# Split tables made once, and the mix as one plain fp32 product of identity plus matrix

## The reference, cut to what matters

```
x: (64 sequences, 32 channels, 512); adapter: (64,), values 2..6; cond: (64,), values 0..15

def lora_add(base, inp, A, B):            # A (16, 16, in), B (16, out, 16), one of 16 adapters per sequence
    Ab, Bb = A[0][adapter], B[0][adapter]
    t = einsum('bri,bni->bnr', Ab, inp)
    return base + einsum('bor,bnr->bno', Bb, t) * 0.5
gate = lora_add(x @ W_gate.T, x, A_gate, B_gate)      # 512 -> 1376
up   = lora_add(x @ W_up.T,   x, A_up,   B_up)
act  = silu(gate) * up
h    = x + lora_add(act @ W_down.T, act, A_down, B_down)   # 1376 -> 512
out  = h + einsum('bct,bcd->bdt', h, weights[cond])   # weights (16, 32, 32): mixes the 32 channels of a sequence
```

## Time and profile before

| | us |
|---|---|
| median of 3 runs | 447.93 (446.21 to 448.08) |
| profiled execution, its own time | 446.79 |
| its span, first to last instruction | 445.0 |
| TensorE busy | 438.1 (98%) |
| VectorE busy | 335.2 (75%) |
| ScalarE busy | 212.3 (48%) |
| POOL (GpSimd) busy | 169.7 (38%) |

### The profile page before, as it was taken

How to read it: one execution, slowest core, us unless ns; L and a number is a source line. 1 busy time by engine, 2 the same in 40 slices (tenths; PEclk the granted TensorE clock), 3 DMA queues, 4 the chain that set the end, 5 groups by cost and what they waited for, 6 DMA issues and landing times.

```text
span 445.0 us, 7248 instructions
## 1 busy us (share of the span) xinstructions
PE 438.1 (98%) x2475; PEld 393.5 (88%) x2475; DVE 335.2 (75%) x623; ACT 212.3 (48%) x397; POOL 169.7 (38%) x156
## 2 busy tenths in 40 slices
PE   8989999999999999999999999999999999999997
PEld 6877888888888888888888888999999999999996
DVE  6779999878867867857857858978667767766665
ACT  6746355366444544543543444843454454444531
POOL 2722223121121221121121452675776666756620
PEclk9999999999999999999999999999999999999999
DMA  8975664356555665665565599947776665556631
GB/s 243 381 242 146 181 172 114 109 172 188 145 181 151 159 172 145 161 173 144 159 173 144 145 287 340 247 138 202 215 201 208 208 180 178 177 178 196 191 96 47
DMA packets 99843, 81.12 MB, mean 182 GB/s; under 512 B 50944, under 2 KB 83200, under 8 KB 99808
## 3 DMA queue, kind: packets, MB, share of 16 engines
q1 hardware_dynamic: 88512, 47.27, 37.9%
q0 software_dynamic: 11008, 33.30, 24.8%
q10 hardware_dynamic: 288, 0.10, 0.1%
HBM read 65.18 MB, written 15.47 MB: 181 GB/s over the span
## 4 chain that ended last, share of the span: by engine, by line
PE 92%; DMA 2%; POOL 2%; issue 2%; DVE 1%; ACT 1%; SPq 0%; POOLq 0%
PE bank L1384 28%; PE bank L1262 9%; PE bank L1263 9%; PE bank L1261 9%; PE bank L1216 7%; PE bank L1217 7%; PE bank L1218 7%; PE bank L1283 4%; PE bank L1284 4%; PE bank L1414 2%; POOL a_raw L453 2%; PE bank L1394 2%; DMA b_raw<-in_b_rows,rows 2%; DMA gu_landing<-in_w_gate 1%; PE bank L1399 1%
## 5 line engine op out<-in xcount | busy, mean ns | idle before, releaser
L453 POOL DMA_INDIRECT b_raw<-in_b_rows,rows x48 | 51.8, 1078 | 188.7 <-DVE b_gu L803 188.1
L1384 PE MATMUL bank<-wd,actT_hi 128*128 128x288 f32 (+1 forms) x636 | 109.9, 295 | 0.0
L1384 PEld LDWEIGHTS bank<-wd,actT_hi 128*128 128x128 f32 (+1 forms) x636 | 93.8, 188 | 1.4 <-issue 0.2
L453 POOL DMA_INDIRECT a_dn_raw<-in_a_dn_rows,rows x64 | 77.3, 1208 | 19.5 <-issue 19.5
L803 DVE SCALAR_TENSOR_TENSOR b_gu<-b_raw,low_rows,b_gu 128x1024 fp32r<-128x1024 f32 (+1 forms) x48 | 55.6, 1159 | 26.8 <-ACT b_gu L513 26.8
L1384 PE MATMUL bank<-wd,actT_lo 128*128 128x288 f32 (+1 forms) x318 | 68.1, 296 | 0.0
L513 ACT ACTIVATE b_gu<-b_raw 128x1024 fp32r<-128x1024 f32 (+1 forms) x48 | 46.2, 963 | 11.2 <-DMA b_raw<-in_b_rows,rows 9.8
L1384 PEld LDWEIGHTS bank<-wd,actT_lo 128*128 128x128 f32 (+1 forms) x318 | 51.0, 188 | 0.0
L603 ACT ACTIVATE act<-bank 128x512 f32<-128x512 f32 (+1 forms) x48 | 26.1, 546 | 41.4 <-PE bank L1284 41.4
L910 DVE TENSOR_TENSOR act<-act,bank 128x512 f32<-128x512 f32 (+1 forms) x48 | 29.8, 621 | 8.6 <-PE bank L1284 7.8
L799 DVE TENSOR_TENSOR actT_lo<-actT_raw,actT_hi 128x1280 fp32r<-128x1280 f32 (+1 forms) x32 | 27.0, 886 | 11.6 <-ACT actT_hi L513 11.6
(11 more groups left out here) (180 smaller groups left out, 1004.2 us busy)
## 6 DMA issues: line engine op xcount, KB each, us to landing
actT_raw<-actT_dram SPq DMA_DIRECT2D x16, 640.0 KB
actT_dram<-staging SPq DMA_DIRECT2D x64, 128.0 KB, 2.9
x_sb<-in_x SPq DMA_DIRECT2D x16, 256.0 KB, 2.9
xT_raw<-in_xT SPq DMA_DIRECT2D x15, 256.0 KB, 2.7
out<-out_sb SPq DMA_DIRECT2D x15, 256.0 KB
a_raw<-in_a_gu_rows SPq DMA_DIRECT2D x56, 64.0 KB, 2.7
actT_dram<-staging SPq DMA_DIRECT2D x32, 88.0 KB, 3.2
wd_raw<-in_w_down SPq DMA_DIRECT2D x10, 256.0 KB, 5.9
```

Of the source, the lines that this page charges most:

```text
L453: return pool.indirect_dma_start(dst, None, src, bass.IndirectOffsetOnAxis(ap=rows[:, tile, col:col + 1], axis=0))
L1384: last = pe.matmul(ps_down[e][half][:, 0:HALF], a[e][0:n, c, :], wd[0:n, c, part, at:at + HALF], start=(c == 0 and i == 0), stop=(c == NC ...
```

## The change

Three tables are made in DRAM while stage one runs. `a_table` has for each adapter's A rows of down the hi part and the lo part side by side (1408 bytes a row), `b_table` has hi rows of B in its first half and lo rows in its second, and `mix_table` has each mix matrix plus the identity. They are made in seven rounds: four for A, two for B, one for mix. A round is a load by SP into `a_dn_raw[0]`, a copy on ScalarE into `a_dn_raw[1]`, a subtraction on VectorE in place, and two stores by SP; the mix round has no copy and adds the identity. Rounds 0 and 1 stand in pair 3, 2 and 3 in pair 4, 4 and 5 in pair 5, 6 in pair 6. The first round of a pair stands before `split_b(pr,2,0)` on ScalarE and VectorE, the second after `split_b(pr,2,1)`. The load of a round waits until the stores of the one before it have landed. The first A gather waits for all stores.

In stage two the A rows of tiles 2 to 15 are gathered from `a_table` into `a_pair` (which lies over `b_raw` and part of `b_gu`) and copied into `wd` by two ScalarE copies; VectorE no longer takes part. B rows are gathered from `b_table` straight into `b_dn`, now double, once `down_lora` of the tile two before is through. The mix matrices are loaded by SP, four DMAs of 32x32 with a register load each, straight onto the diagonal blocks of `mix_w`. The mix is one plain fp32 product of `mix_w` and the unsplit h in `x_sb`; its result is out itself, which ScalarE copies to `out_sb` (`copy_out`). The mask's minus sign is turned at the start of stage two.

```diff
+A_ROUNDS = ADAPTERS // TILE_SEQS
+ROUNDS = A_ROUNDS + 3
+FIRST_ROUNDS = 3
...
+    a_table = nc.dram_tensor("a_table", (ADAPTERS * P, 2 * A_DN), F32, kind="Internal").ap()
+    b_table = nc.dram_tensor("b_table", (2 * ADAPTERS * RANK, H), F32, kind="Internal").ap()
+    mix_table = nc.dram_tensor("mix_table", (ADAPTERS * CH, CH), F32, kind="Internal").ap()
...
+        with ExitStack() as then:
+            a_pair = [sb(f"a_pair{e}", [P, TILE_SEQS, 2 * A_DN], F32, then) for e in range(2)]
...
-        mix_raw = [sb(f"mix_raw{e}", [P, CH]) for e in range(2)]
-        mix_hi = sb("mix_hi", [P, P], F32R)
-        mix_lo = sb("mix_lo", [P, P], F32R)
+        mix_raw = sb("mix_raw", [P, CH])
+        mix_w = [sb(f"mix_w{e}", [P, P]) for e in range(2)]
...
+        b_dn = [sb(f"b_dn{e}", [P, H], F32R) for e in range(2)]
...
+        def table_parts(i):
+
+            if i < A_ROUNDS:
+                raw, to = slice(0, TILE_SEQS * A_DN), slice(TILE_SEQS * i * P, TILE_SEQS * (i + 1) * P)
+                return raw, [a_table[to, part * A_DN:(part + 1) * A_DN].rearrange("(a p) n -> p a n", p=P)
+                             for part in range(2)]
+            if i < A_ROUNDS + 2:
+                r0 = (i - A_ROUNDS) * P
+                return slice(0, H), [b_table[part * ADAPTERS * RANK + r0:part * ADAPTERS * RANK + r0 + P, :]
+                                     for part in range(2)]
+            return slice(0, TILE_SEQS * CH), [mix_table.rearrange("(a p) n -> p a n", p=P)]
...
+        def rounds_of(pr):
+
+            return [i for i in (2 * (pr - FIRST_ROUNDS), 2 * (pr - FIRST_ROUNDS) + 1) if 0 <= i < ROUNDS]
...
+            def load_round(i):
+                reached(sp, tables_stored, 32 * i)
+                if i < A_ROUNDS:
+                    sp.dma_start(a_dn_raw[0][:, :, :], a_round(i)).then_inc(table_landed, 16)
+                elif i < A_ROUNDS + 2:
+                    r0 = (i - A_ROUNDS) * P
+                    sp.dma_start(table_sb(0, slice(0, H)), b_dn_rows[r0:r0 + P, :]).then_inc(table_landed, 16)
+                else:
+                    sp.dma_start(table_sb(0, slice(0, TILE_SEQS * CH), CH),
+                                 mix_rows.rearrange("(a p) n -> p a n", p=P)).then_inc(table_landed, 16)
+                    sp.dma_start(table_sb(0, slice(TILE_SEQS * CH, (TILE_SEQS + 1) * CH)), eye)\
+                        .then_inc(table_landed, 16)
+
+            def store_round(i):
+                cols, tables = table_parts(i)
+                n = A_DN if i < A_ROUNDS else H if i < A_ROUNDS + 2 else CH
+                sp.wait_ge(table_ready, i + 1)
+                for part, to in enumerate(tables):
+                    src = table_sb(1 - part if i < ROUNDS - 1 else 0, cols, n if len(to.shape) == 3 else None)
+                    sp.dma_start(to, src).then_inc(tables_stored, 16)
+
+            def load_mix(m, e):
+                reached(sp, mix_done, 2 * (m - 1))
+                for q in range(TILE_SEQS):
+                    r = slice(q * CH, (q + 1) * CH)
+                    col = 2 * TILE_SEQS + 2
+                    row = sp.value_load(rows[q * CH:q * CH + 1, m, col:col + 1], min_val=0, max_val=(ADAPTERS - 1) * CH)
+                    sp.dma_start(mix_w[e][r, r], mix_table[bass.ds(row, CH), :]).then_inc(mix_landed[e], 16)
...
+                if rounds:
+                    load_round(rounds[0])
...
                     spill(pr, s)
+                    if s < len(rounds):
+                        store_round(rounds[s])
+                    if s + 1 < len(rounds):
+                        load_round(rounds[s + 1])
...
             sp.wait_ge(s_used, FAST)
             load_x(0, 0)
             load_actT(2, 0)
+            sp.wait_ge(tables_stored, 32 * ROUNDS - 16)
+            load_mix(0, 0)
             load_x(1, 1)
             load_actT(3, 1)
+            load_mix(1, 1)
...
+                if m == 0 and q0 == 0:
+                    pool.wait_ge(tables_stored, 32 * ROUNDS - 16)
+                if m == 2:
+                    for t in range(2):
+                        pool.wait_ge(section_done[t], NS * PAIRS)
+                reached(pool, a_dn_copied, m - 3)
                 for q in range(q0, q1):
-                    gather(a_dn_raw[m % 2][:, q, :], a_dn_rows, m, TILE_SEQS + 1 + q).then_inc(a_dn_landed[m % 2], 16)
+                    to, table = (a_dn_raw, a_dn_rows) if m < 2 else (a_pair, a_table)
+                    gather(to[m % 2][:, q, :], table, m, TILE_SEQS + 1 + q).then_inc(a_dn_landed[m % 2], 16)
...
+                reached(pool, down_lora_done, 2 * (m - 1))
+                gather(b_dn[m % 2][:, :].bitcast(F32), b_table, m, 2 * TILE_SEQS + 1).then_inc(b_dn_landed[m % 2], 16)
...
+            gather_b_dn(1)
             for m in range(2, TILES):
                 gather_a_dn(m)
-                pool.wait_ge(down_done, m - 1)
-                gather_b_dn(m - 1)
-                gather_mix(m - 1)
-            gather_b_dn(TILES - 1)
-            gather_mix(TILES - 1)
+                gather_b_dn(m)
...
+            def split_round(i):
+
+                if i == ROUNDS - 1:
+                    return
+                sc.wait_ge(table_landed, 16 * (i + 1))
+                cols, _ = table_parts(i)
+                hi(table_sb(1, cols).bitcast(F32R), table_sb(0, cols)).then_inc(table_hi_ready, 1)
...
                 split_b(pr, 2, 1)
+                for i in rounds_of(pr)[1:2]:
+                    split_round(i)
...
+                    for part in range(2):
+                        of = a_pair[e][:, :, part * A_DN:(part + 1) * A_DN]
+                        last = hi(wd_a(part, e), of.rearrange("p q (c r) -> p q c r", c=NC))
+                    last.then_inc(a_dn_copied, 1)
...
+            def copy_out(m, e):
+                sc.wait_ge(mix_done, 2 * (m + 1))
+                reached(sc, stored[e], 16 * (m // 2))
+                hi(out_sb[e][:, :], ps_mix[:, 0:H]).then_inc(out_ready, 1)
...
                 split_td(2 * j - 1)
-                split_mix(2 * j - 1, 1)
-                if j == 1:
-                    split_h(2 * j - 1, 1)
-                    split_a_dn(2 * j + 1, 1)
-                else:
-                    split_a_dn(2 * j + 1, 1)
-                    split_h(2 * j - 1, 1)
+                split_a_dn(2 * j + 1, 1)
                 split_actT(2 * j + 1, 1)
-                split_b_dn(2 * j, 0)
+                copy_out(2 * j - 1, 1)
                 split_td(2 * j)
-                split_mix(2 * j, 0)
                 split_a_dn(2 * j + 2, 0)
-                split_h(2 * j, 0)
                 split_actT(2 * j + 2, 0)
-                split_b_dn(2 * j + 1, 1)
+                copy_out(2 * j, 0)
...
+            def split_round(i):
+
+                if i == ROUNDS - 1:
+                    ve.wait_ge(table_landed, 16 * (ROUNDS + 1))
+                    to = table_sb(0, slice(0, TILE_SEQS * CH), CH)
+                    ones_ = a_dn_raw[0][:, 0:1, TILE_SEQS * CH:(TILE_SEQS + 1) * CH]
+                    nc.vector.tensor_tensor(to, to, ones_.to_broadcast([P, TILE_SEQS, CH]), ALU.add)\
+                        .then_inc(table_ready, 1)
+                    return
+                cols, _ = table_parts(i)
+                ve.wait_ge(table_hi_ready, i + 1)
+                lo(table_sb(0, cols).bitcast(F32R), table_sb(0, cols), table_sb(1, cols)).then_inc(table_ready, 1)
...
                 add_u7(pr, 1)
+                for i in rounds_of(pr)[0:1]:
+                    split_round(i)
                 split_b(pr, 2, 0)
                 if not last:
                     split_a(pr + 1, 0)
@@ -1008,12 +1084,14 @@
                 if not last:
                     split_x(pr + 1, 1)
                 split_b(pr, 2, 1)
+                for i in rounds_of(pr)[1:2]:
+                    split_round(i)
                 if not last:
                     sum_x(pr + 1)
...
+            def turn_mask():
+
+                for q in range(TILE_SEQS):
+                    c = 2 * q * RANK
+                    last = nc.vector.memset(mask[q * CH:(q + 1) * CH, c:c + RANK], LORA_SCALE)
+                last.then_inc(mask_turned, 1)
+                ve.wait_ge(mask_turned, 1)
...
-                                            ALU.add).then_inc(h_summed, 1)
-                for half, (cols, at) in enumerate(down_halves(e)):
-                    ve.wait_ge(h_hi_ready, 2 * m + half + 1)
-                    lo(h_lo[:, cols], x_sb[e][:, cols], h_hi[:, cols]).then_inc(h_ready, 1)
...
+                                            ALU.add).then_inc(h_ready, 1)
...
-            def mix_products(out_, cols):
-                pe.matmul(out_, mix_hi[:, :], h_hi[:, cols], start=True, stop=False)
-                pe.matmul(out_, mix_lo[:, :], h_hi[:, cols], start=False, stop=False)
-                return pe.matmul(out_, mix_hi[:, :], h_lo[:, cols], start=False, stop=True)
-
             def mix(m):
-                pe.wait_ge(mix_ready, m + 1)
+                e = m % 2
```

(5 more changed lines are left out.)

141 lines of the change are left out of this document (49 added, 92 removed).

## The result

| us | before | after |
|---|---|---|
| median of runs on one chip | 447.72 (446.21 to 448.08, 4 runs) | 462.23 (460.06 to 462.55, 4 runs) |
| profiled execution, its own time | 446.79 | 460.06 |
| its span | 445.0 | 458.0 |

The ratio after to before is 1.0326, 95% interval 1.0289 to 1.0364: slower. The forecast was 459.9, range 451 to 468. The profiled execution is the fastest of the kernel after, with a mean granted clock of 0.999; its others have spans of 460.2 to 461.2 us at 0.992 to 0.996. The medians are 14.5 us apart and the two profiled spans 13.0; the profiles can account for the 13.0.

A forecast was written before the change was run, and what follows sets the result against it. TensorE was taken to bound the kernel. Mix 2.7, table-round stalls 8.25 and down-stage start 1.0 made 12.0 us on the profiled 446.79, so 458.8; the median lies 1.1 above, giving 459.9 us, range 451 to 468.

The forecast's parts named there:

- The bound: Whole kernel: TensorE, busy 98% of the span, sets the time; work taken off VectorE and ScalarE gives nothing back.
- The mix: Down tiles: one plain fp32 product for three single-pass ones, +0.16 to +0.20 us a tile, +2.7 us over fifteen tiles.
- Slot A at zero: First round of a pair, before split_b(pr,2,0): its load lands before VectorE comes, 2.0 us of cover, cost 0.
- Slot B, three stalls: Second round of pairs 3, 4, 5: waiting for stores, then load, stalls the next pair's lora 3.3, 3.3, 1.65 us; +8.25 us.
- T: Moment the second round's table load lands in pair 3, 151.7; b ready at 160.4, stall T - 148.4 = 3.3 us.
- The wait at tile 2: Start of the down stage: fourth A gather 1.25 us later, b_dn(1) put in front; stall 0 to 2.0, taken as +1.0 us.
- The steady down stage at zero: Later down tiles: removed work lies beside TensorE, added gathers and DMAs are hidden; slack 2.1 us, cost 0.
- a sign of being wrong: Down stage: the forecast is wrong if ScalarE waits for a_pair in each tile and TensorE behind it.
- Hidden rounds: Gate/up pairs: landing is short or VectorE makes up more, so the table rounds cost nothing; 450.9 us, chance 0.13.
- late gathers: Down stage: gathers land 3 us later than taken, 0.9 over the slack on 13 tiles; about 12 us more, 472; chance 0.10.
- the third rival: Down stage: 288-column matmul spacing shrinks as ScalarE and VectorE traffic goes, 12 us back; 439 with rounds hidden; chance 0.05.

The follow-up runs named there:

- experiment 1: Kernel after without the load, copy and subtraction of each pair's second round, its stores kept and issued with the first round's: 455.74 us, ratio to before 1.0162.
- experiment 4: Kernel after with each pair's second round moved into the next pair, its stores ahead of load_a: 460.10 us; with 32 unused words 458.20; SP's queue also split, 455.23 and 454.09.
- experiment 5: Kernel after with the gather of b_dn(1) issued behind tile 2's A-row gathers and nothing else changed: 465.22 us, one execution.

## Why the prediction was right, point by point

**The bound.** Right: TensorE sets the time throughout, and 49 us less VectorE work bought nothing.

**The mix.** Predicted 0.16 to 0.20 per tile, 2.7 in all. The chain of a down tile after answers to the earlier trace rows:

```profile
324.61 0.49 PE bank L1445 x4
325.11 3.17 PE bank L1435 x24
328.28 0.86 PE bank L1453 x2
329.14 5.57 PE bank L1435 x42
334.71 0.48 PE bank L1445 x4
```

The mix takes 0.86 instead of 0.70, the doubled rate of the earlier trace rows without the 0.04 that I added for instruction starts; over the whole stage tiles are 10.09 us apart instead of 9.92. So it is 0.16 to 0.17 per tile and 2.4 to 2.5 in all, the low end of my bounds. Alone on the kernel before it measured 1.8 by the ratio, 2.5 by the span.

**Slot A at zero.** Right, and shown by experiment 1. It stayed true only while its load landed ahead of VectorE; in experiment 4 it did not.

**Slot B, three stalls.** The mechanism is the predicted one, row by row. Pair 3 begins 1.10 us later than before, so in the frame of before T is 152.70 - 1.10 = 151.6; predicted 151.7. Its two parts were each off by 0.6 to 0.7, in opposite directions: the store leg took 3.8 (4.5 predicted), the load leg 4.0 (3.4). That T comes out to 0.1 us is partly luck. b was ready at 161.37 - 1.10 = 160.3 (160.4). The stall beyond a quiet pair is 2.94, not 3.3, since the quiet pair is itself 0.5 longer; with the forms put back it is 3.18. The term that was mis-sized is pair 5's, 0.40 for 1.65. There SP's rows are

```profile
217.78 0.81 SPq L404 DMA_DIRECT2D b_table<-a_dn_raw  x2
220.45 0.34 SPq L391 DMA_DIRECT2D a_dn_raw<-in_b_dn_rows  x1
```

and the copy starts at 223.57: two legs of 2.7 and 3.1, 2.0 us less than the A rounds' 7.8, where I had taken 0.9 less for the smaller transfers. The A rounds also store in pieces of 704 bytes and the B rounds in pieces of 2 KB; whether that is the difference was not tried. Sum 6.3 for 8.25.

The Trainium skill, page DMA: Bandwidth & Descriptors, section Anatomy of one DMA, has about 2.0 us plus bytes at 436 GB/s, in a section on DMAs that GpSimd issues (these two are SyncE's). By it T was 150.3 and the stalls 4.4. The A legs were slower than that by 1.3 us, and the stalls, 6.3, lie between its figure and mine.

**The wait at tile 2.** Predicted +1.0 (0 to 2.0), measured 0.72, and 0.9 to 2.0 in the five variants of the kernel after that keep the order of the gathers. The price is right. In all of these the fourth A gather leaves 11.4 us after the first b_dn gather and TensorE is through with tile 1 at 19.8; what differs is the time from that gather to ScalarE's copy, 4.7 us in the kernel after and 4.9 to 5.9 in the others, within the 3.7 to 5.9 of the earlier trace rows. The reason given for the later gather, b_dn(1) ahead of it, is not right: experiment 5 takes it away and nothing is won. By the rows of POOL what makes it late is the wait of the first A gather for the last lora product together with POOL's hold; no run separates the two.

**The steady down stage at zero.** Right, with less room than the prediction gave it. ScalarE waits for A rows in nearly every tile, 31.0 us over 13 waits, which I had named as a sign of being wrong if TensorE waited behind it; it does not. ScalarE's and VectorE's rows in the tile that begins 18 matmuls (2.4 us) before its lora, at 322.2, and POOL's row, to be held against the earlier trace rows, in the one that begins at 342.4:

```profile
326.80 1.48 ACT L584 ACTIVATE wd<-a_pair 128x704 fp32r<-128x704 f32 x2 [3.56 <-DMA a_pair<-a_table,rows]
```

```profile
329.67 1.69 DVE L860 TENSOR_TENSOR actT_lo<-actT_raw,actT_hi 128x1280 fp32r<-128x1280 f32 x2 [3.98 <-ACT actT_hi L584]
```

```profile
351.88 0.95 POOL L525 DMA_INDIRECT a_pair<-a_table,rows  x1 [0.30 <-issue]
```

The subtraction ends at 331.36 and the next tile begins at 332.3: slack 0.9, not 2.1, since the last gather of a tile's rows goes out 9.5 us into it and not 8.1.

**What no step of it had.** The 128-byte shift, 3.5 us of the span after. I read that edit (`mix_raw` one buffer instead of two) as a change of buffers only and gave it no price. The total came out near because this missing +3.5 (0.6 in pair 1, 2.9 in pairs 2 to 7) met slot B's -2.0, the mix's -0.3 and tile 2's -0.3: 13.0 on the profiled span against 12.0, and 14.5 between the medians. That they nearly cancel is luck in part. The shift and slot B's term are not independent: with the forms put back, slot B's stalls grow to 8.7, so that the forecast's 8.25 fits the kernel without the shift better, and the measured time is the same.

**The rivals.** Hidden rounds fell with the two pairs of 36.5 us; late gathers with the steady 10.09; the spacing of the 288-column products, which the third rival wanted to shrink, stayed (42 of them in 5.57 us, before 5.55), and that of the 512-column products grew, for a reason that was not in it. The Trainium skill, page TensorE: Matmul & The Clock Gate, section Back-to-back issue gap, gives the N/2.4 + 2.5 ns that the prediction sets beside this rival for a matmul by itself, and says of a stream with weight loads that both set the spacing. So the 10 ns above it were no sign of foreign traffic, and taking 49 us of VectorE's work away did not bring them back.

No variant beats the kernel before. The nearest with the whole change in it is 1.5% above it (454.09 median): the plain fp32 mix, tile 2 and 0.6 us in the pairs are what is left of the change in its profile, beside the dip at the start, which variants of the kernel before have too.

## What to carry to other kernels

Work taken off engines that run beside the bound buys nothing; what a change adds to their queues can still cost, by a single wait with other work behind it. Price such a wait by the whole dependent chain (store landed, load landed, copy, and everything queued behind on the same engine) against the moment at which the bounding engine wants the result, and recheck the loads that were free after every move in a shared queue. Before believing a small difference, compare start-to-start spacing of identical instructions: a buffer added or dropped moves all tiles behind it.

## What the runs showed of the hardware that was not expected

- The spacing of 512-column single-pass products with a weight load each was 227 ns or 232 ns depending on where the tiles behind one buffer lie relative to those ahead of it; 128 bytes up or down gave the slow one, 256 up or all tiles together the fast one (up, 256 and all together in one execution each). Products whose own operands had not moved were slowed as well (227 to 231). On a pair of 100 such products it is 0.49 us, on the kernel 0.6% (1.0062 [1.0036, 1.0087]). Products of 480 columns and fewer kept theirs.
- POOL was held some 5 us soon after a pause of 10 us, ending 8.6 us after its first gather, in all 14 profiles.
- After some 3 us with few matmuls, TensorE's granted clock was 0.50 for 3.4 us (from 314.7 in the kernel with the moved gather). Eight of 14 profiles also have such a stretch from 28 or 29 us on, after one in which TensorE was idle part of the time; in these pair 1 begins at 48.3 to 49.0 us, in the others at 47.0 to 47.7.
